# Mamba block on one core: one scan of 1024 columns for both channel blocks of a unit

## The reference, cut to what matters

```
delta = softplus(dlt @ W_dt.T + b_dt)
A = -jnp.exp(A_log)
deltaA = jnp.exp(delta[..., None] * A)
deltaBx = delta[..., None] * Bm[:, :, None, :] * xc[..., None]
h = deltaA * h + deltaBx            # step by step over the tokens
y = einsum('bdn,bn->bd', h, c)      # summed over the 16 states
```

## Time and profile before

| | |
|---|---|
| median of 3 runs | 5888.44 us (5884.67 to 5889.52) |
| profiled execution | 5896.29 us, span 5894.5 us |
| busy over the span | PE 84%, DVE 85%, POOL 71%, ACT 48% |
| scan stage | about 160 to 4110 us |
| mean granted PE clock | 0.925 of full |

### The profile page before, as it was taken

One profiled execution on the slowest core, in us unless ns is written; L12 is line 12 of the kernel. 1 busy time (PEld: TensorE's weight loads), 2 busy tenths in 40 slices (PEclk: granted clock), 3 DMA queues, 4 the chain that ended last, 5 costly groups with the idle time before them and its releaser, 6 DMA issues. The chain is left out here.

```text
span 5894.5 us, 80810 instructions
## 1 busy us (share of the span) xinstructions
PE 4944.5 (84%) x21894; PEld 3377.2 (57%) x21894; DVE 5038.6 (85%) x5901; ACT 2808.4 (48%) x6398; POOL 4166.9 (71%) x2410
## 2 busy tenths in 40 slices
PE   7678797787878878788788887875399999999999
PEld 3445454454544545445454454443278888888887
DVE  1899899898989999899999999987878888888887
ACT  2666666666666666666666666652211111111111
POOL 0899999999999999999999999996522222222221
PEclk9899998998989989899898998976599999999999
DMA  2455554555555555555555555543100000000010
GB/s 102 152 165 170 160 182 165 162 174 161 182 160 165 172 161 185 161 169 171 161 181 163 168 170 161 176 143 118 54 22 32 32 32 30 30 30 32 32 32 25
DMA packets 394632, 728.62 MB, mean 124 GB/s; under 512 B 44052, under 2 KB 44180, under 8 KB 394103
## 3 DMA queue, kind: packets, MB, share of 16 engines
q1 hardware_dynamic: 394230, 724.19, 38.9%
HBM read 689.41 MB, written 34.61 MB: 123 GB/s over the span
## 5 line engine op out<-in xcount | busy, mean ns | idle before, releaser
L525 POOL TENSOR_TENSOR slot<-du,b_row 128x1024 f32<-128x1024 f32 x1024 | 2419.9, 2366 | 3.0 <-DMA b_row<-b_c_rows 1.5
L768 DVE TENSOR_TENSOR_SCAN decay<-decay,state,slot 128x512 f32<-128x512 f32 x1024 | 1314.8, 1284 | 283.7 <-ACT decay L684 169.0
L533 POOL TENSOR_TENSOR slot<-slot,c_row 128x512 f32<-128x512 f32 x960 | 1226.3, 1277 | 168.2 <-ACT state L672 168.0
L890 PE MATMUL y_ps<-ident,slot 128*128 128x128 f32 x8192 | 1099.7, 285 | 182.8 <-POOL slot L533 172.9
L890 PEld LDWEIGHTS y_ps<-ident,slot 128*128 128x128 f32 x8192 | 986.0, 148 | 433.5 <-POOL slot L533 217.1
L774 DVE TENSOR_TENSOR_SCAN slot<-decay,state,slot 128x512 f32<-128x512 f32 x960 | 1210.5, 1261 | 0.0
L829 PE MATMUL work_ps<-h_t,win 128*128 128x512 f32 x2048 | 1006.4, 637 | 162.3 <-DVE delta L738 96.4
L1242 POOL TENSOR_TENSOR hq<-hid,qinv 128x1408 f32<-128x1408 f32 x64 | 166.3, 2599 | 1240.0 <-DVE qinv L1269 1240.0
L829 PEld LDWEIGHTS work_ps<-h_t,win 128*128 128x128 f32 x2048 | 399.7, 204 | 625.2 <-issue 472.7
L681 ACT ACTIVATE decay<-delta,rate 128x512 f32<-128x512 f32 x1024 | 703.8, 687 | 2.1
L684 ACT ACTIVATE decay<-delta,rate 128x512 f32<-128x512 f32 x1024 | 699.5, 683 | 0.0
(11 more groups left out here) (192 smaller groups left out, 7854.6 us busy)
## 6 DMA issues: line engine op xcount, KB each, us to landing
b_row<-b_c_rows SPq DMA_DIRECT2D x1024, 256.0 KB, 3.7
c_row<-b_c_rows SPq DMA_DIRECT2D x1024, 256.0 KB, 3.4
win<-in_w_in SPq DMA_DIRECT2D x256, 256.0 KB, 2.9
xt<-in_x SPq DMA_DIRECT2D x16, 1024.0 KB, 6.3
xr<-in_x SPq DMA_DIRECT2D x64, 256.0 KB, 5.2
x_after_mamba<-xr SPq DMA_DIRECT2D x64, 256.0 KB, 2.6
xa<-x_after_mamba SPq DMA_DIRECT2D x64, 256.0 KB, 2.8
xres<-x_after_mamba SPq DMA_DIRECT2D x64, 256.0 KB, 2.7
```

Of the source, the lines that this page charges most:

```text
L525: pool.tensor_tensor(slot[:, u % SLOTS, :, :], du[:, p % 2, :, :], b_row[:, u % BC_RING, :].unsqueeze(1).to_broadcast((P, 2, T)), ALU.mult ...
L533: pool.tensor_tensor(h, h, c_row[:, u % BC_RING, :], ALU.mult).then_inc(S["c1_pool"], 1)
L768: dve.tensor_tensor_scan(d, d, slot[:, u % SLOTS, 0, :], state[:, 2 * p, n:n + 1], ALU.mult, ALU.add).then_inc(S["scan0_done"], 1)
L890: op = pe.matmul(y_ps[i][:, s, :], slot[:, u % SLOTS, i, s * P:(s + 1) * P], ident[:, :], is_transpose=True, start=False, stop=(n == N - 1 ...
```

## The change

The two scans of a unit become one over 1024 columns: block 0's 512 columns, then block 1's. A scan has only one start value. So that block 1 starts from its own state, the first column of block 1 gets a decay of exactly zero, which forgets block 0, and decay times old state is added to the input there beforehand.

- Zero decay: once `du` has used delta, ACT overwrites delta's first column of block 1 by 1e30 (`lead_exp`), after it has taken the real decays of that column for the 16 states (one 128x16 exponential). The exponential of 1e30 times a negative rate is zero; the rate is clamped at -1e-20 so that it is never zero.
- State at the seam: DVE multiplies these 16 decays by the 16 saved states (`lead_mul`, 128x16), once per pair, so four times a chunk. ACT adds the result of state n to the first input column of block 1 in every unit (`lead_in`, one column).
- C product: both blocks by one engine in one instruction of 1024 columns. DVE does it for 37 of the 64 units (`DVE_C`), directly behind the scan, from PSUM into the slot; POOL for the other 27, in place in the slot, still two units later. For POOL's units the scan writes into the slot, for DVE's into the decay buffer.
- `save_states` copies both last columns in one instruction. The decays of unit u wait for it only if DVE multiplied unit u - 2.
- PE waits for the whole C product of a unit; one semaphore per slot of the C ring tells both PE and SP.
- All step tables and the assignment of PSUM banks (`BANK`) are rewritten; the pieces in them are the same, with the new ones added: `lead` at ACT positions 11, 27, 46 and 63, `du` at POOL positions 11, 26, 46 and 63, `lead_mul` on DVE at (13, 1), (28, 1), (46, 1) and, for the next chunk, (62, 0). Here (pos, 0) stands behind the scan and (pos, 1) behind the C product. The silu pieces stand at 26 and 52 (before 16 and 50).

```
-DVE_C = (7, 23, 39, 55,)
+
+DVE_C = (
+    0, 2, 4, 6, 7, 9, 11, 13, 14, 16, 18, 20, 21, 23, 25, 26, 28, 30, 32, 33, 35, 37, 39, 40, 42, 44, 45, 47, 49, 51,
+    52, 54, 56, 58, 59, 61, 63,
+)
...
-                        dve.tensor_scalar(rate[:, :, :], rate[:, :, :], -1.0, None, ALU.mult)
+                        dve.tensor_scalar(rate[:, :, :], rate[:, :, :], -1.0, -1e-20, ALU.mult, ALU.min)
...
-            decay = [[ps(f"decay{k}_{i}", [P, T]) for i in range(2)] for k in range(2)]
+            decay = [ps(f"decay{k}", [P, 2, T]) for k in range(2)]
...
-            def c1_done(u, c):
-
-                mine = [v for v in range(UNITS) if (v in DVE_C) == (u in DVE_C)]
-                return S["c1_dve" if u in DVE_C else "c1_pool"], c.at(len(mine), mine.index(u) + 1)
+            def c_done(u, c):
+
+                return c_row_used[u % BC_RING], c.at(UNITS // BC_RING, u // BC_RING + 1)
+
+            def flat(ap):
+                return ap.rearrange("p a t -> p (a t)")
+
+            def two(row):
+                return row.unsqueeze(1).to_broadcast((P, 2, T))
...
-                    def times_c1(u, c):
-                        h = slot[:, u % SLOTS, 1, :]
-                        wait(pool, S["state1_saved"], c.at(UNITS, u + 1))
+                                           two(b_row[:, u % BC_RING, :]), ALU.mult).then_inc(S["ub_ready"], 1)
+
+                    def times_c(u, c):
+                        h = slot[:, u % SLOTS, :, :]
+                        wait(pool, S["state_saved"], c.at(UNITS, u + 1))
                         wait(pool, *ring_loaded(c_loaded, c, u))
-                        pool.tensor_tensor(h, h, c_row[:, u % BC_RING, :], ALU.mult).then_inc(S["c1_pool"], 1)
+                        pool.tensor_tensor(h, h, two(c_row[:, u % BC_RING, :]), ALU.mult).then_inc(c_row_used[u % BC_RING], 1)
...
+                    def lead_exp(p, c):
+
+                        first = delta[:, p % 2, 1, 0:1]
+                        wait(act, S["u_ready"], c.at(PAIRS, p + 1))
+                        wait(act, S["lead_ready"], c.at(PAIRS, p - 1))
+                        act.activation(lead_decay[:, p % 2, :], rate[:, 2 * p + 1, :], ACT.Exp, scale=first).then_inc(S["lead_exp"], 1)
+                        wait(act, S["lead_exp"], c.at(PAIRS, p + 1))
+                        act.activation(first, huge[:, :], ACT.Copy).then_inc(S["lead_cut"], 1)
...
-                        wait(act, S["c0_done"], c.at(UNITS, u + 1))
-                        act.activation(state[:, 2 * p, n:n + 1], decay[u % 2][0][:, T - 1:T], ACT.Copy).then_inc(S["state0_saved"], 1)
+                        h = decay[u % 2] if u in DVE_C else slot[:, u % SLOTS, :, :]
                         if u in DVE_C:
-                            wait(act, *c1_done(u, c))
-                            h_end = decay[u % 2][1][:, T - 1:T]
+                            wait(act, *c_done(u, c))
                         else:
-                            wait(act, S["scan1_done"], c.at(UNITS, u + 1))
-                            h_end = slot[:, u % SLOTS, 1, T - 1:T]
-                        act.activation(state[:, 2 * p + 1, n:n + 1], h_end, ACT.Copy).then_inc(S["state1_saved"], 1)
+                            wait(act, S["scan_done"], c.at(UNITS, u + 1))
+                        act.activation(state[:, 2 * p:2 * p + 2, n], h[:, :, T - 1], ACT.Copy).then_inc(S["state_saved"], 1)
...
+                            wait(act, S["lead_cut"], c.at(PAIRS, p + 1))
                         v, cc = back(c, u - 2)
-                        if v in DVE_C:
-                            wait(act, S["state1_saved"], c.at(UNITS, u - 1))
-                        act.activation(decay[u % 2][1][:, :], delta[:, p % 2, 1, :], ACT.Exp,
-                                       scale=rate[:, 2 * p + 1, n:n + 1]).then_inc(S["decay_ready"], 1)
-                        wait(act, S["state0_saved"], c.at(UNITS, u - 1))
-                        act.activation(decay[u % 2][0][:, :], delta[:, p % 2, 0, :], ACT.Exp,
-                                       scale=rate[:, 2 * p, n:n + 1]).then_inc(S["decay_ready"], 1)
+                        if exists(cc) and v in DVE_C:
+                            wait(act, S["state_saved"], c.at(UNITS, u - 1))
+                        for i in (1, 0):
+                            act.activation(decay[u % 2][:, i, :], delta[:, p % 2, i, :], ACT.Exp,
+                                           scale=rate[:, 2 * p + i, n:n + 1]).then_inc(S["decay_ready"], 1)
+
+                    def lead_in(u, c):
+                        p, n = divmod(u, N)
+                        first = slot[:, u % SLOTS, 1, 0:1]
+                        if n == 0:
+                            wait(act, S["lead_ready"], c.at(PAIRS, p + 1))
+                        wait(act, S["ub_ready"], c.at(UNITS, u + 1))
+                        act.activation(first, first, ACT.Identity, bias=lead[:, p % 2, n:n + 1]).then_inc(S["u_led"], 1)
...
+                                lead_in(pos, c)
...
+                    def lead_mul(p, c):
+
+                        wait(dve, S["lead_exp"], c.at(PAIRS, p + 1))
+                        wait(dve, S["state_saved"], c.at(UNITS, N * (p + 1) - UNITS))
+                        wait(dve, S["u_led"], c.at(UNITS, N * (p - 1)))
+                        dve.tensor_tensor(lead[:, p % 2, :], lead_decay[:, p % 2, :], state[:, 2 * p + 1, :],
+                                          ALU.mult).then_inc(S["lead_ready"], 1)
...
-                    def scan0(u, c):
+                    def scan(u, c):
                         p, n = divmod(u, N)
                         if n == 0:
-                            wait(dve, S["state0_saved"], c.at(UNITS, N * (p + 1) - UNITS))
-                            wait(dve, S["state1_saved"], c.at(UNITS, N * (p + 1) - UNITS))
+                            wait(dve, S["state_saved"], c.at(UNITS, N * (p + 1) - UNITS))
                         wait(dve, S["decay_ready"], c.at(2 * UNITS, 2 * u + 2))
-                        wait(dve, S["ub_ready"], c.at(UNITS, u + 1))
-                        d = decay[u % 2][0][:, :]
-                        dve.tensor_tensor_scan(d, d, slot[:, u % SLOTS, 0, :], state[:, 2 * p, n:n + 1],
-                                               ALU.mult, ALU.add).then_inc(S["scan0_done"], 1)
-
-                    def scan1(u, c):
-                        p, n = divmod(u, N)
-                        d, h = decay[u % 2][1][:, :], slot[:, u % SLOTS, 1, :]
-                        dve.tensor_tensor_scan(d if u in DVE_C else h, d, h, state[:, 2 * p + 1, n:n + 1],
-                                               ALU.mult, ALU.add).then_inc(S["scan1_done"], 1)
+                        wait(dve, S["u_led"], c.at(UNITS, u + 1))
+                        d, h = flat(decay[u % 2][:, :, :]), flat(slot[:, u % SLOTS, :, :])
+                        dve.tensor_tensor_scan(d if u in DVE_C else h, d, h, state[:, 2 * p, n:n + 1],
+                                               ALU.mult, ALU.add).then_inc(S["scan_done"], 1)
 
                     def times_c(u, c):
                         wait(dve, *ring_loaded(c_loaded, c, u))
-                        wait(dve, S["scan0_done"], c.at(UNITS, u + 1))
-                        dve.tensor_tensor(slot[:, u % SLOTS, 0, :], decay[u % 2][0][:, :], c_row[:, u % BC_RING, :],
-                                          ALU.mult).then_inc(S["c0_done"], 1)
-                        if u in DVE_C:
-                            wait(dve, S["scan1_done"], c.at(UNITS, u + 1))
-                            dve.tensor_tensor(slot[:, u % SLOTS, 1, :], decay[u % 2][1][:, :], c_row[:, u % BC_RING, :],
-                                              ALU.mult).then_inc(S["c1_dve"], 1)
+                        wait(dve, S["scan_done"], c.at(UNITS, u + 1))
+                        dve.tensor_tensor(slot[:, u % SLOTS, :, :], decay[u % 2][:, :, :], two(c_row[:, u % BC_RING, :]),
+                                          ALU.mult).then_inc(c_row_used[u % BC_RING], 1)
...
-                                scan0(pos, c)
+                                scan(pos, c)
                             for step, arg, cc in steps(DVE_STEPS, c, (pos, 0)):
                                 HAVE[step](arg, cc)
-                            if exists(c):
-                                scan1(pos, c)
+                            if exists(c) and pos in DVE_C:
+                                times_c(pos, c)
...
+                        wait(pe, *c_done(u, c))
                         for i in range(2):
-                            if i == 0:
-                                wait(pe, S["c0_done"], c.at(UNITS, u + 1))
-                            else:
-                                wait(pe, *c1_done(u, c))
```

(36 more changed lines are left out.)

65 lines of the change are left out of this document (17 added, 48 removed), and 32 rows, old and new, of tables (BANK, PE_STEPS).

## The result

The changed kernel takes 5906.8 us (median of 7 runs, 5899.6 to 5913.2) against 5889.4: a ratio of 1.0028, 95% interval 1.0017 to 1.0040. It is slower by 17 us, a small loss but clear of the noise, where 0.7% faster was forecast with a range of 5700 to 5970. The profiled execution took 5906.8 us over a span of 5905.0.

What follows compares the result with a forecast made beforehand. Neither engine alone: POOL's work is the floor, ACT's queue adds. After: DVE work 223.3, idle 10.4 + 6.0 + 0.6, period 240.3 against 242.85, -2.55 x 16 = -41 us, so 5847 us, 0.7% faster; range 5700 to 5970.

Steps and rivals of the forecast that it cites:

- The 1024-column scan: DVE's joint scan: 2.26 us instead of two halves at 1.19, 7.7 us a chunk less; range 0 to -7.7.
- the whole number of column times: DVE's scan step taken as two product-column times of 1.04 ns, with 0.12 us paid once, so 2.26 us.
- DVE's work without the lead products: DVE's summed work of 223.3 us a chunk, less lead_mul's 0.9 of work and 4.7 of blocking by POOL.
- PE and SP ... both are costed at nothing: PE's later C-product waits and SP's C-row loads: hidden by slots and lead, 0 us; upper bound 1.1 us on some units.
- idle for POOL 6.6 falls to about 0.6: DVE's idle per chunk waiting for POOL's B product: 6.6 us falls to about 0.6, as POOL has less work.
- the 10.4 kept for ACT: DVE's idle waiting for ACT's decays: stays at 10.4 us a chunk, the longer ACT chain costed at nothing more.
- for PE and softplus 6.0 kept: DVE's idle for PE's residual inputs (3.1 us) and smaller rows (2.9 us): stays at 6.0 us a chunk.
- the delay behind the product's own scan: DVE's 37 C products each directly follow their own scan: 0.12 us each, +4.4 us a chunk; range 0 to 4.4.
- the terms carried over: DVE's present idle per chunk by cause: 10.4 us ACT, 6.6 POOL, 6.0 PE and softplus, 23.0 in all.
- the lead product: DVE's lead_mul waits 0 to 2.36 us for one POOL instruction; half taken, 4 x 1.2 = +4.7 us a chunk.
- The ACT rival: Hand-over through ACT becomes the bound: decay waits grow, softplus pieces add; slower, 5922 to 5973, put at 5945 us; 19%.
- Full relief of POOL: Rival: POOL still sets the pace with its present idle, 231.6 us a chunk, -180 us, 5708 us; 17%.

Runs made afterwards that it cites:

- the fold: Changed kernel, but ACT's seam addition also multiplies old state by the lead decay and DVE's lead product goes: 5883.0 us.
- two scans: Changed kernel with two 512-column scans, each from its own state, and no seam work: 5861.8 us; with SP's waiting steps moved later as well, 5785.3 us.
- the repaired kernel: Changed kernel with DVE's lead product folded into ACT's seam addition and SP's waiting weight loads and residual saves moved later: 5775.0 us.
- the run with later SP steps: Changed kernel with only SP's table altered, its waiting weight loads and residual saves moved later: 5919.8 us.

## Why the prediction was wrong, by its own steps

**Right.** The 1024-column scan: 2348 and 2342 ns recorded, where 2.33 to 2.36 us was said. A column costs (2348 - 1284)/512 = 2.08 ns, and some 0.2 us is paid once per record; the whole number of column times held. POOL's whole C product: 2363 ns for 2.36. DVE's C product at 1222. DVE's work without the lead products was summed to 223.3 - 5.6 = 217.7 us a chunk; in the run with the fold it is 0.890 of 242.7, or 216.1. POOL's was put at 220.3 and measured 221.9. DVE and POOL did become nearly equally full, at 0.900 and 0.910. The next start 2.26 us behind a scan's came as said (1860.50 and 1862.76 in the changed kernel's timeline).

**Failed: the step "PE and SP ... both are costed at nothing".** I took POOL's 1.1 us of waiting for rows before as cover for a table of SP steps that was rewritten, and named only the C row's wait, not the weight loads and saves that stand in the same queue. They hold SP 438 us longer in 3,000, and POOL waits 10.0 us a chunk for B rows, slightly more than its relief of 9.6. In POOL's own account this is the term that was missing: 221.9 of work (220.3 said) and 22.0 idle, of which 10.3 is for the saved state, as before (10.5), and 10.0 for B rows. Moving these steps gave 76 us beside two scans and 108 (5883.0 to 5775.0) beside the fold. Those 108 us are well over the 17 by which the change lost, and over the 60 by which the forecast missed.

**Right in size, wrong in its path: "idle for POOL 6.6 falls to about 0.6".** With the 10.4 kept for ACT the sum had 11.0 us a chunk before the scan; the idle there is 8.5 and names ACT's seam addition. But ACT itself stood there for POOL (15.5 a chunk), so POOL's lateness still reached DVE under another name; with punctual rows and the fold it is 4.9. The addition also takes 287 ns, not 0.2; ACT's busy time rose by 170.3 - 153.2 = 17 us a chunk.

**Failed: "for PE and softplus 6.0 kept".** In DVE's account this is the term that is off: of the period of 243.9, 219.5 is work (223.3 said) and 8.5 the seam, which leaves 15.9 where 6.0 stood. Residuals rose from 3.1 to 5.2 us a chunk, gates waiting for PE take 2.6, softplus waiting for ACT 1.9, late C rows 2.0 and the lead exponentials 1.0; the last two the sum had put at nothing. Another 2.6 are short gaps before C products, most of them, by my reading, the delay behind the product's own scan, which the sum had inside the work (4.4). The longer waits for PE are hardly the clock's doing: the granted clock of the two windows was 0.92, and 0.93 before, and in the repaired kernel the residuals wait still longer, 100.4 us of 3,000, at a clock of 0.94. What lengthens them was not tested.

**A slip in the sum.** The period before, 242.85, holds 23.5 us of DVE's idle, but the terms carried over add to 23.0. The half microsecond that fell out is 8 us of the 41 that were forecast.

**Wrong in form, small in this kernel: the lead product.** I bounded its wait by one POOL instruction, 2.36 us, and took 4 x 1.2 us a chunk. In the changed kernel it cost less, 60.8 us over the run for the 90 that this sum had, and one product of 64 broke the bound, with 10.00 us. With rows on time it broke at 23 places, 15 of them near 8.8 us, and the same products unused cost 159 us of time. Why they are let in sooner while the rows are late is open. Behind unit 46 gaps of POOL are not the reason: in 13 of the 15 chunks after the first POOL's next instruction followed there without one in the changed kernel. The two faults hid each other; that is why neither repair alone showed much.

**The rivals.** The ACT rival named 5945 and has its share: taking the hand-over away gives 32 us in the changed kernel and 43 in the repaired one. It was not the main term. Full relief of POOL (5708) was not reached by any kernel that computes everything; the repaired one has 235.8 us a chunk, (3677.7 - 141.1)/15, where 231.6 had been named.

```profile
L614 ACT ACTIVATE xc<-xc x16: 3616/3627/3642, 141.1 to 3677.7; 128x4096 f32<-128x4096 f32 x16
```

The joint scan itself, the heart of the change, is worth little: 5775.0 against 5785.3 us with two scans, ratios 0.9814 and 0.9819 whose intervals overlap. It saves 53 us where nothing hands over (5785.3 to 5732.4) and gives 43 back to the hand-over. The gain over the kernel before, 1.9%, comes from the whole C products with the new tables and punctual rows; how much of it the tables alone would have given is not separated here. What the tables' fit to the pattern of 37 rests on stays open, as does why the same products are passed over in the joint-scan kernel (3.28 us in the mean) and mostly let in beside two scans (1.56), behind unit 46 each time within 2.01 us.

## What to carry to other kernels

When a table of steps is rewritten, price the transfer queue like an engine: for each step in it that waits, look at what stands behind and when that is wanted, even if today's trace shows no wait for it. A small vector operation with both operands in SBUF can cost far more than its length beside a busy POOL, and the price hangs on where it meets POOL's instructions. Giving it to ACT removed it here; putting one operand in PSUM was not tried for it, but DVE's C products, which have one there, kept their 1.22 us beside the same POOL. When a repair shows nothing, look at what new wait has taken its place before dropping it: here two repairs that gave +13 and -24 us alone gave -132 together.

## What the runs showed of the hardware that was not expected

- A 16-column DVE product with two SBUF inputs waited through several POOL instructions in a row, between 8.66 and 8.84 us at 15 of the 64 places in the run with later SP steps and once 9.96 us, not just until the end of the one under way. At each of these 16 places POOL then stood over 7 us for a state that waited for DVE. Other products of that run were let in at the end of the one instruction that they met (2.08 us at the turn of a chunk), though POOL went on without a gap. Which of the two happens was not found.
- ACT's one-column Identity with a bias from SBUF takes 287 ns in the mean (277 to 302), against means of 169 and 202 for its copies of two columns; with a scale from SBUF as well, in the fold, 378.
- One scan over a pair of decay buffers, 1024 columns of PSUM, shows no price for passing from the first to the second: the added 512 columns cost 2348 - 1284 = 1064 ns, 2.08 each, twice the 1.04 of a product's column that the prediction worked out.
